# Expert stage: one more up-weight load on SyncE, and the last half's rows sent one tile earlier

## The chip, the cores and the metric

The kernel runs on one core of a Trainium2 chip. The metric is the device time of one execution in microseconds (us). Three executions of the kernel before took 436.18, 436.92 and 437.71 us, so the median is 436.92 us.

## What is computed

A transformer layer in float32 on x of 4 x 1024 rows by 128: causal attention with 16 heads and a latent of 32, a layer norm over x plus the attention, then a mixture of eight experts where each row goes to one expert only, and a second layer norm.

```python
x = _layernorm(x + attention(x))
gate_logits = einsum('bsd,ed->bse', x, gate_w) + gate_b + expert_bias
top_idx = argmax(gate_logits)
for e in range(8):
    h = relu(x @ w1[e] + b1[e])            # 128 -> 512
    y = h @ w2[e] + b2[e]                  # 512 -> 128
    out += (top_idx == e) * y
x = _layernorm(x + out)
```

## The kernel before

The engines run programs of their own, joined by semaphores: PE (TensorE), DVE (VectorE), ACT (ScalarE), POOL (GpSimd) and SP (SyncE, which only issues DMAs).

**Attention stage.** The loop over 144 units (`u`, 36 for each of the four batches) computes scores on PE, exponentials on ACT and clips on DVE. Between the units stand jobs for one half batch (512 rows) each: the output projection (`out`), the first layer norm and a transpose (`turnx`), the gate (`gate`) and `rank`, which gives each row its place in its expert's region of the DRAM tensor `by_expert`. After `rank`, POOL's `route` (L585) waits for `index_ready` and scatters the 512 rows of the half to `by_expert` with four indirect DMAs of 128 rows (L591).

**Expert stage.** It works through TILES = 39 tiles of 128 rows of one expert. The first EARLY_TILES = 17 tiles hold only rows of the first seven halves, so they need no row of the last half. The last half's own jobs (`out`, `turnx`, `gate`, `rank`) run inside the expert loop, at tiles 2, 5, 6 and 7 (`TAIL_AT`). The late tiles, 17 to 38, need all that follows from it: the four scatters of the last half, eight pad blocks written behind the regions (`pad`, L403: six by SP, two by ACT at tiles 8 and 9) and DVE's late plan of the tiles (tiles 7, 8, 9).

For tile `c`:

- SP's `load_tile` (L529, DMA at L535) fetches the 128 rows to one of 12 buffers `xs`; from tile 12 on it waits until the result of tile `c - 12` has been written.
- The up weights of the tile's expert (256 KB) go to one of six buffers `w1_tile`. In the kernel before, SP fetches those of tiles 0 to 4 during the attention stage (L539 to L542), ahead of its row loads, and ACT those of tile 5 on, five tiles ahead, with `load_up` (L1115, DMA at L1121): a value load of the expert's number, a wait for the buffer, the DMA.
- PE's loop at step `c` (L1381): `up_rows(c)` (L1350), `turn_x(c + 2)` (L1340), `down_rows(c - 1)` (L1367), then the tail job of that step.
- ACT's loop at step `c` (L1141): `relu(c)` (four activations, L1133), `xT_evac(c + 2)` (L1111), `load_up(c + 5)`, the tail job, and at steps 8 and 9 one pad. At step 0 it also empties the last attention sum (L1079). `relu` does the value load itself if `load_up` has not done it for that tile.
- DVE's loop (L1015): `residual` (L980), `y_sum` (L987), statistics (L993), `y_norm(c - 2)` (L1008), moments (L999, L1001), tail jobs, late plan.
- POOL's loop at step `c` (L622): `y_inverse_std(c - 1)` (L610), `write(c - 2)` (an indirect DMA to `out`, L618), and the routes that `ROUTE_AT` gives to this step. Each is in program order.

SP's order in the expert stage is: its five weight loads, row loads 0 to 16, six pads, the wait for all scatters, pads and the late plan (L546 to L549), row loads 17 to 38.

Of the kernel before, what the change touches and what calls it, by code (L numbers as in the profile page):

```python
# [126 lines left out]
def sums(b, pair, qc):  # L127
    return (b * PAIRS + pair) * NQC + qc
# [6 lines left out]
PLAN_AT = (7, 8, 9)  # L135

EARLY_PLAN_AT = (23, 24, 27, 28)
ROUTE_AT = {8: (0, 1), 9: (2, 3)}
PAD_AT = 8
PADS_ACT = 2  # L140
LAST_HALF = B * NQC - 1
# [2 lines left out]
def tail_job(c, kind=None):  # L144


    return [job for job in TAIL_JOBS if TAIL_AT.get(c) == job[0] and kind in (None, job[0])]
# [28 lines left out]
TILES = N // P + E - 1  # L176
# [5 lines left out]
W1_SLOTS = 6  # L182
W1_AHEAD = W1_SLOTS - 1
# [10 lines left out]
def build(nc, io):  # L194
    ctx = ExitStack()
    with ctx:
# [174 lines left out]
        def prob_ap(u, seg):  # L371
            _, _, off, w = seg
            return prob[u % P_SLOTS][:, :, off:off + w]
# [22 lines left out]
        def pad(eng, experts):  # L396


            eng.wait_ge(pad_ready, 1)
            eng.wait_ge(pad_in, 16)  # L400
            for e in experts:
                at = eng.value_load(pad_at[0:1, e:e + 1], min_val=0, max_val=DUMMY)
                eng.dma_start(by_expert[bass.ds(at, P), :], pad_row[:]).then_inc(padded, 16)  # L403
# [35 lines left out]
        def _(sp):  # L439
# [96 lines left out]

            sp.wait_ge(weighted, (B - 1) * UB)
            sp.wait_ge(scored, 2 * ((B - 1) * UB + NU))
            for c in range(W1_AHEAD):  # L539
                e = sp.value_load(expert_tab[0:1, c:c + 1], min_val=0, max_val=E - 1)  # L540
                sp.dma_start(w1_tile[c], io["w1"].rearrange("e d f -> (e d) f")[bass.ds(e * D, D), :]
                             ).then_inc(w1_in[c], 16)  # L542
# [11 lines left out]
        def _(pool):  # L554
# [15 lines left out]
            def inverse_std(g):  # L570
                pool.wait_ge(var_ready, g + 1)
                pool.tensor_tensor(rstd[g % Q][:], var_eps[g % Q][:], const[:, CONST["half"]], ALU.pow  # L572
                                   ).then_inc(rstd_ready, 1)
# [11 lines left out]
            def route(g, tiles):  # L585

                q = g % Q
                pool.wait_ge(index_ready, g + 1)
                pool.sem_inc(pool_seen, 1)
                for t in tiles:  # L590
                    pool.indirect_dma_start(by_expert, bass.IndirectOffsetOnAxis(ap=index[q][:, t:t + 1], axis=0),  # L591
                                            xrow[q][:, t, :], None).then_inc(routed[q], 16)
# [29 lines left out]
            for c in range(TILES + 2):  # L622
# [4 lines left out]
                if TAIL_AT.get(c) == "out":  # L627
                    inverse_std(LAST_HALF)
                if c in ROUTE_AT:
                    route(LAST_HALF, ROUTE_AT[c])  # L630
            for i in range(RING):
# [3 lines left out]
        def _(dve):  # L635
# [55 lines left out]
            def clip(u):  # L691

                _, segs = segments(u)
                p = prob[u % P_SLOTS]
                diag = UNITS[u % NU][1][0][1] * P >= UNITS[u % NU][0] * QC
                dve.wait_ge(exped, 2 * u + 2)
                if not diag:
                    dve.tensor_scalar(p[:], p[:], P_HI, P_LO, ALU.min, ALU.max).then_inc(clipped, 1)  # L698
                    return
                widths = [w for _, _, _, w in segs]  # L700
                if widths == [QC]:
                    on, off = p[:, :, 0:P], p[:, :, P:QC]
                    mask = mask_hi[:, 0, :].unsqueeze(1).to_broadcast([P, HG, P])
                elif widths == [P, 3 * P]:
                    on, off = p[:, :, 0:2 * P], p[:, :, 2 * P:QC]
                    mask = mask_hi[:].rearrange("p i q -> p (i q)").unsqueeze(1).to_broadcast([P, HG, 2 * P])
                else:
                    both = p[:].rearrange("p h (i s) -> p (h i) s", i=2)
                    on, off = both[:, :, 0:P], both[:, :, P:2 * P]
                    mask = mask_hi[:, 0, :].unsqueeze(1).to_broadcast([P, 2 * HG, P])  # L710
                dve.tensor_scalar(off, off, P_HI, P_LO, ALU.min, ALU.max)  # L711
                dve.scalar_tensor_tensor(out=on, in0=on, scalar=P_LO, in1=mask, op0=ALU.max, op1=ALU.min  # L712
                                         ).then_inc(clipped, 1)
# [327 lines left out]
        def _(act):  # L1041
# [32 lines left out]
            def o_evac(k):  # L1074

                act.wait_ge(weighted, last_unit(k) + 1)
                if k >= 2:
                    act.wait_ge(o_turned, k - 1)
                act.activation(o_sb[k % 2][:], o_acc[:], ACT.Copy).then_inc(o_out, 1)  # L1079

            def job(kind, i):
                if kind == "v":
                    v_evac(i)
                if kind == "turnx":
                    act.wait_ge(turnx_mm, i + 1)
                    act.activation(flipped[i % Q][:], misc[:], ACT.Copy).then_inc(turnx_out, 1)
# [19 lines left out]
            def xT_evac(c):  # L1106
                act.wait_ge(xs_turned, c + 1)
                if c >= 2:

                    act.wait_ge(up_mm, c - 1)  # L1110
                act.activation(xsT[c % 2][:], bank[c % 2][:, 0:P], ACT.Copy).then_inc(xsT_ready, 1)  # L1111
# [3 lines left out]
            def load_up(c):  # L1115


                experts[c] = act.value_load(expert_tab[0:1, c:c + 1], min_val=0, max_val=E - 1)
                if c >= W1_SLOTS:
                    act.wait_ge(up_mm, c - W1_SLOTS + 1)  # L1120
                act.dma_start(w1_tile[c % W1_SLOTS],  # L1121
                              io["w1"].rearrange("e d f -> (e d) f")[bass.ds(experts[c] * D, D), :]
                              ).then_inc(w1_in[c % W1_SLOTS], 16)

            def relu(c):

                e = experts.pop(c) if c in experts else act.value_load(expert_tab[0:1, c:c + 1], min_val=0, max_val=E - 1)
                act.wait_ge(up_mm, c + 1)
                if c >= 2:
                    act.wait_ge(down_mm, c - 1)  # L1130
                for f in range(DFF // P):
                    t = slice(f * P, (f + 1) * P)
                    last = act.activation(hiddenT[c % 2][:, t], bank[4 + c % 2][:, t], ACT.Relu,  # L1133
                                          bias=b1T[:, bass.ds(e * (DFF // P) + f, 1)])
                last.then_inc(hiddenT_ready, 1)
# [5 lines left out]
            for c in range(TILES):  # L1141
                relu(c)
                if c == 0:
                    o_evac(sums(B - 1, 1, 1))
                if c + 2 < TILES:
                    xT_evac(c + 2)
                if c + W1_AHEAD == EARLY_TILES:
                    act.wait_ge(planned, 4)
                if c + W1_AHEAD < TILES:
                    load_up(c + W1_AHEAD)  # L1150
                for kind, i in tail_job(c):
                    job(kind, i)
                if PAD_AT <= c < PAD_AT + PADS_ACT:
                    pad(act, [E - PADS_ACT + c - PAD_AT])
# [346 lines left out]
```

## Time and profile before

| | |
|---|---|
| median of three executions | 436.92 us |
| profiled execution, its own time | 439.81 us |
| its span (first to last instruction) | 438.1 us |
| PE busy | 406.7 us, 93% |
| DVE busy | 373.8 us, 85% |
| ACT busy | 351.6 us, 80% |
| POOL busy | 173.1 us, 40% |
| mean granted clock of PE | 0.977 |

The profiled execution lies 2.9 us above the median, and 1.7 us of it lie outside its span. Times within the trace are microseconds from the start of the span. A row of the timeline gives the start, the duration, the engine, the line of the program, the operation, output <- input and the number of instructions; the bracket gives the idle time of the engine before it and what ended it. `SPq` and `ACTq` are the DMA-issuing instructions of SP and ACT. The attention stage ends at about 341 us, the expert stage begins with the transposes at 338 us.

### The profile page before, as it was taken

To read this page: it belongs to the slowest core of one execution; us is meant where nothing else is said; L and a number is where in the kernel's file an instruction comes from. 1 tells how busy PE (TensorE), PEld (TensorE's weight loads), DVE (VectorE), ACT (ScalarE), POOL (GpSimd) and SP (SyncE) were. 2 spreads that over 40 slices of the span, in tenths; PEclk is the share of its full clock that TensorE was granted. 3 is DMA by queue.
4 is the path that set the end of the run, shared out by engine and by line. 5 is a ranking of instruction groups with operands and counts; after the bars stand their busy time and mean duration, and the time that the engine had idled before them with its cause. 6 is when DMAs were issued, how large, how long until landed. Compare 5 with 4: busy or idle time off the path is not lost. (4 is left out here: it accounts for less than half of the span.)

```text
span 438.1 us, 12095 instructions
## 1 busy us (share of the span) xinstructions
PE 406.7 (93%) x4139; PEld 222.8 (51%) x4139; DVE 373.8 (85%) x816; ACT 351.6 (80%) x560; POOL 173.1 (40%) x164
## 2 busy tenths in 40 slices
PE   8899999999999999899999999999998798699993
PEld 5533344444434354344344444343343697699993
DVE  3979799999999999979999999999998687367674
ACT  3879999999889989798899999989986464366662
POOL 8221001331553022507601322454001576678887
PEclk9889999999999999899999999999999999799998
DMA  5268501676066155401940760067214456567640
GB/s 154 54 170 196 155 1 49 145 176 194 2 160 181 49 114 125 104 1 30 211 101 1 170 151 21 2 145 197 72 41 121 116 156 173 145 175 214 189 139 19
DMA packets 33004, 50.60 MB, mean 116 GB/s; under 512 B 5627, under 2 KB 16545, under 8 KB 32944
## 3 DMA queue, kind: packets, MB, share of 16 engines
q1 hardware_dynamic: 25488, 36.51, 33.7%
q10 hardware_dynamic: 5184, 9.05, 7.2%
q0 software_dynamic: 2272, 4.27, 3.0%
q8 instruction: 34, 0.56, 0.5%
q14 instruction: 26, 0.21, 0.2%
HBM read 21.35 MB, written 5.33 MB: 61 GB/s over the span
## 5 line engine op out<-in xcount | busy, mean ns | idle before, releaser
L1048 ACT ACTIVATE prob<-ring 128x1024 f32<-128x1024 f32 x288 | 273.1, 1047 | 26.3 <-PE ring L1237 25.2
L1255 PE MATMUL o_acc<-prob,v_stat 128*32 128x512 f32 (+3 forms) x1536 | 156.0, 502 | 6.5 <-ACT o_sb L1079 5.1
L1237 PE MATMUL ring<-queries,keys 32*128 32x512 f32 (+3 forms) x1536 | 129.0, 384 | 3.6 <-DVE whole_q L658 3.0
L1237 PEld LDWEIGHTS ring<-queries,keys 32*128 32x128 f32 x1536 | 72.3, 186 | 88.7 <-issue 48.1
L698 DVE TENSOR_SCALAR prob<-prob 128x2048 f32<-128x2048 f32 x64 | 77.4, 1219 | 4.9 <-ACT prob L1048 4.6
L712 DVE SCALAR_TENSOR_TENSOR prob<-prob,mask_hi 128x1024 f32<-128x1024 f32 (+1 forms) x80 | 81.0, 1013 | 0.0
L1133 ACT ACTIVATE prob<-ring,b1T 128x128 f32<-128x128 f32 x156 | 44.5, 368 | 39.2 <-issue 17.8
L711 DVE TENSOR_SCALAR prob<-prob 128x1024 f32<-128x1024 f32 (+1 forms) x80 | 64.9, 811 | 4.0 <-ACT prob L1048 4.0
L1255 PEld LDWEIGHTS o_acc<-prob,v_stat 128*32 128x32 f32 x1536 | 34.4, 109 | 61.6 <-issue 42.4
L591 POOL DMA_INDIRECT by_expert<-xrow,index x32 | 43.5, 1360 | 46.0 <-DVE index L809 38.4
L572 POOL TENSOR_TENSOR rstd<-var_eps,const 128x4 f32<-128x4 f32 x8 | 17.1, 2134 | 92.4 <-DVE var_eps L757 92.4
L1367 PE MATMUL ring<-w,prob 128*128 x312 | 43.7, 285 | 7.8 <-ACT prob L1133 6.5
L581 POOL CAST key_parts<-whole_k 128x512 fp32r<-128x512 f32 x15 | 13.1, 875 | 87.6 <-ACT whole_k L1072 87.6
L1367 PEld LDWEIGHTS ring<-w,prob 128*128 128x128 f32 x312 | 39.6, 199 | 9.2 <-issue 9.1
L618 POOL DMA_INDIRECT out<-prob,queries x39 | 40.5, 1039 | 8.7 <-issue 8.7
L1350 PE MATMUL ring<-prob,v_stat 128*128 128x128 f32 x312 | 43.0, 282 | 0.3
L1350 PEld LDWEIGHTS ring<-prob,v_stat 128*128 128x128 f32 x312 | 38.9, 196 | 1.6 <-issue 1.6
L583 POOL CAST query_parts<-whole_q 128x512 fp32r<-128x512 f32 x15 | 29.1, 1939 | 12.8 <-DVE whole_q L658 12.8
L610 POOL TENSOR_TENSOR y_rstd<-y_var,const 128x1 f32<-128x1 f32 x39 | 22.9, 588 | 12.6 <-DVE y_var L1001 10.9
L993 DVE BATCH_NORM_STATS2 y_stats<-prob 128x6 f32<-128x128 f32 x39 | 11.5, 295 | 13.1 <-DVE prob L987 11.8
L987 DVE TENSOR_TENSOR prob<-ring,prob 128x128 f32<-128x128 f32 x39 | 11.3, 290 | 12.4 <-remote 6.2
L1202 PE MATMUL ring<-latent,w_kq 64*128 64x512 f32 x60 | 17.9, 674 | 0.9 <-DVE whole_q L667 0.5
(114 smaller groups left out, 330.2 us busy)
## 6 DMA issues: line engine op xcount, KB each, us to landing
queries<-query_parts SPq DMA_DIRECT2D x60, 256.0 KB, 4.0
v_stat<-in_w ACTq DMA_DIRECT2D x34, 256.0 KB
keys<-key_parts SPq DMA_DIRECT2D x60, 128.0 KB, 2.4
queries<-by_expert SPq DMA_DIRECT2D x39, 66.0 KB
xrow<-in_x_rows SPq DMA_DIRECT2D x8, 264.0 KB, 4.7
xT<-in_x_T SPq DMA_DIRECT2D x8, 256.0 KB, 3.1
v_stat<-in_w SPq DMA_DIRECT2D x5, 256.0 KB
out<-prob,queries POOLq DMA_INDIRECT x39
```

The source lines that it names most:

```text
L583: pool.tensor_copy(query_parts[i % 2][:, 0, :], whole_q[i % 2][:]).then_inc(upper_queries, 1)
L591: pool.indirect_dma_start(by_expert, bass.IndirectOffsetOnAxis(ap=index[q][:, t:t + 1], axis=0), xrow[q][:, t, :], None).then_inc(routed[q ...
L618: pool.indirect_dma_start(io["out"], bass.IndirectOffsetOnAxis(ap=xs[c % RING][:, D:D + 1].bitcast(U32), axis=0), zs[c % RING][:], None, b ...
L698: dve.tensor_scalar(p[:], p[:], P_HI, P_LO, ALU.min, ALU.max).then_inc(clipped, 1)
L711: dve.tensor_scalar(off, off, P_HI, P_LO, ALU.min, ALU.max)
L712: dve.scalar_tensor_tensor(out=on, in0=on, scalar=P_LO, in1=mask, op0=ALU.max, op1=ALU.min).then_inc(clipped, 1)
L1048: act.activation(prob[u % P_SLOTS][:, 2 * half:2 * half + 2, :].rearrange("p h s -> p (h s)"), slot(("score", u, half))[:], ACT.Exp, scale ...
L1133: last = act.activation(hiddenT[c % 2][:, t], bank[4 + c % 2][:, t], ACT.Relu, bias=b1T[:, bass.ds(e * (DFF // P) + f, 1)])
L1237: last = pe.matmul(out[:, j % 2 * QC + off:j % 2 * QC + off + w], keys[hg][r, kt * P:(kt + 1) * P], queries[hg][r, qc, part, QC - w:QC], s ...
L1255: last = pe.matmul(o_acc[j * VW:(j + 1) * VW, QC - w:QC], v_stat[b % 2][:, hg, kt, j, :], prob[u % P_SLOTS][:, j, off:off + w], start=begi ...
L1350: last = pe.matmul(bank[4 + c % 2][:, t], w1_tile[c % W1_SLOTS][:, t], xsT[c % 2][:], start=True, stop=True)
L1367: last = pe.matmul(bank[2 + c % 2][:, 0:D], hiddenT[c % 2][:, f * P:(f + 1) * P], w2_cols[:, bass.ds(e * DFF + f * D, D)], start=f == 0, s ...
```

## The change

SP fetches the up weights of six tiles (0 to 5) instead of five, ahead of its row loads. ACT's first `load_up` is that of tile 6, at step 1; at step 0 it issues none, and `relu(5)` does its own value load. POOL issues the last half's scatters 0 and 1 at step 7 and 2 and 3 at step 8, instead of steps 8 and 9. Nothing else is touched.

```diff
-ROUTE_AT = {8: (0, 1), 9: (2, 3)}
+ROUTE_AT = {7: (0, 1), 8: (2, 3)}
...
             sp.wait_ge(weighted, (B - 1) * UB)
             sp.wait_ge(scored, 2 * ((B - 1) * UB + NU))
-            for c in range(W1_AHEAD):
+            for c in range(W1_SLOTS):
                 e = sp.value_load(expert_tab[0:1, c:c + 1], min_val=0, max_val=E - 1)
                 sp.dma_start(w1_tile[c], io["w1"].rearrange("e d f -> (e d) f")[bass.ds(e * D, D), :]
                              ).then_inc(w1_in[c], 16)
...
                 if c + W1_AHEAD == EARLY_TILES:
                     act.wait_ge(planned, 4)
-                if c + W1_AHEAD < TILES:
+                if W1_SLOTS <= c + W1_AHEAD < TILES:
                     load_up(c + W1_AHEAD)
```

with W1_SLOTS = 6 and W1_AHEAD = 5.

## Rows read from the trace of the kernel before

**Rows 1.** Busy time by stretch: stretch, length, engines (instructions), granted clock, DMA share, GB/s

```profile
344.81:346.84 2.03, 0.00 (x0) 0.00 (x0) 0.63 (x3) 1.27 (x5) 0.33 (x1) 1.00 0.68 188
374.80:378.37 3.57, 0.00 (x1) 0.01 (x1) 1.07 (x6) 1.28 (x5) 1.31 (x2) 0.83 0.55 149
378.37:384.00 5.63, 5.63 (x26) 5.63 (x27) 2.85 (x14) 2.64 (x11) 4.85 (x6) 0.50 0.53 155
384.00:426.00 42.00, 42.00 (x376) 42.00 (x375) 29.26 (x132) 28.31 (x109) 34.36 (x44) 1.00 0.64 185
```

**Rows 2.** Timeline of PE and ACT at the start of the expert stage

```profile
341.67 1.13 PE L1350 MATMUL ring<-prob,v_stat 128*128 128x128 f32 x8
342.16 0.30 ACT L1111 ACTIVATE prob<-ring 128x128 f32<-128x128 f32 x1
342.83 2.04 ACTq L1121 DMA_DIRECT2D v_stat<-in_w  x1
344.54 0.27 PE L1340 MATMUL ring<-ident,queries 128*128 128x128 f32 x1
345.57 1.14 ACT L1133 ACTIVATE prob<-ring,b1T 128x128 f32<-128x128 f32 x4 [3.11 <-issue]
346.85 1.15 PE L1367 MATMUL ring<-w,prob 128*128 x8 [2.04 <-ACT prob L1133]
```

**Rows 3.** Line L1121, ACT's weight loads: duration in ns, minimum/median/maximum

```profile
L1121 ACTq DMA_DIRECT2D v_stat<-in_w x34: 14/344/2036, 342.8 to 420.6; - x34
```

**Rows 4.** Timeline of PE, ACT and DVE at steps 13 to 15

```profile
371.42 0.29 DVE L980 TENSOR_TENSOR prob<-queries,rope_q 128x128 f32<-128x128 f32 x1
373.55 1.13 PE L1350 MATMUL ring<-prob,v_stat 128*128 128x128 f32 x8
376.90 0.29 DVE L987 TENSOR_TENSOR prob<-ring,prob 128x128 f32<-128x128 f32 x1 [5.19 <-remote]
377.09 1.14 ACT L1133 ACTIVATE prob<-ring,b1T 128x128 f32<-128x128 f32 x4 [4.82 <-remote]
378.37 2.07 PE L1367 MATMUL ring<-w,prob 128*128 x8 [3.58 <-ACT prob L1133]
380.23 1.91 PE L1350 MATMUL ring<-prob,v_stat 128*128 128x128 f32 x8
384.82 0.27 PE L1340 MATMUL ring<-ident,queries 128*128 128x128 f32 x1
```

**Rows 5.** Timeline of POOL from its step 7 to its step 9

```profile
362.87 1.03 POOL L618 DMA_INDIRECT out<-prob,queries  x1 [0.26 <-issue]
365.68 0.57 POOL L610 TENSOR_TENSOR y_rstd<-y_var,const 128x1 f32<-128x1 f32 x1 [1.78 <-DVE y_var L1001]
367.85 1.02 POOL L591 DMA_INDIRECT by_expert<-xrow,index  x1 [0.30 <-issue]
370.15 0.58 POOL L610 TENSOR_TENSOR y_rstd<-y_var,const 128x1 f32<-128x1 f32 x1
373.52 0.96 POOL L591 DMA_INDIRECT by_expert<-xrow,index  x1 [0.30 <-issue]
```

**Rows 6.** Timeline of SP's pads and of its first late row load

```profile
365.92 0.37 SPq L403 DMA_DIRECT2D by_expert<-pad_row  x1
367.08 0.72 SPq L403 DMA_DIRECT2D by_expert<-pad_row  x1
...
376.85 0.33 SPq L403 DMA_DIRECT2D by_expert<-pad_row  x1
379.38 0.36 SPq L535 DMA_DIRECT2D queries<-by_expert  x1
```

**Rows 7.** SP's waits, and the register moves of line L403 in ns

```profile
SPq L548 <- DMA by_expert<-pad_row: 1.3, 1, 1.3
L403 SPq MOVE by_expert<-pad_row x6: 3/18/722, 365.9 to 376.8; - x6
```

**Rows 8.** Timeline: SP's early weight and row loads, PE's first transposes

```profile
325.62 5.19 SPq L541 DMA_DIRECT2D v_stat<-in_w  x5
331.58 33.50 SPq L535 DMA_DIRECT2D queries<-by_expert  x17
337.99 0.44 PE L1340 MATMUL ring<-ident,queries 128*128 128x128 f32 x2
```

**Rows 9.** All 32 scatters of L591, in ns; DVE's clip from the page; an index

```profile
L591 POOL DMA_INDIRECT by_expert<-xrow,index x32: 958/1322/2101, 94.2 to 373.5; - x32
L698 DVE TENSOR_SCALAR prob<-prob 128x2048 f32<-128x2048 f32 x64 | 77.4, 1219 | 4.9 <-ACT prob L1048 4.6
362.62 0.17 DVE L809 CAST index<-place_of 128x4 uint32<-128x4 f32 x1
```

## Prediction: what the change will do to the time

> **What bounds the kernel now.** I read the busy time by stretch first, then the timelines of single engines inside the stretches where PE is not full. From 384 to 426 us PE is busy without a gap at full clock, while ACT, DVE and POOL are busy for 67 to 82% of the time [rows 1]. So the late expert tiles are bound by PE: whatever time PE gains or loses before tile 17 reaches the end of the kernel in full. Two stretches ahead of that are empty on PE: 2.03 us at 344.81 and 3.57 us at 374.80 [rows 1]. The second is followed by 5.63 us of full work at half the granted clock, 0.50, the 1.2 GHz level [rows 1]. Only these two gaps and the clock behind the second can be won by a change at this place.
>
> The first gap ends when ACT has done `relu(1)`. ACT was not computing before that: it issued the weight load of tile 5, which took 2.04 us, and `relu(1)` could only start at 345.57 [rows 2]. The second gap ends with ACT's `relu(12)` at 377.09; DVE starts again at 376.90 [rows 4]. Both had their inputs long before (DVE stood for 5.19 us). In the same time SP's pads hardly move: the first two start 1.16 us apart, the sixth only at 376.85, and a mere register move of SP takes up to 722 ns [rows 6, 7]. So the sequencers of SP, ACT and DVE run slowly together while scatters, pads and loads are in flight, and no row says which of them does it. I cannot tell whether this slow stretch is as long in executions without the profiler; the profiled one is 439.81 us, 2.89 above the median. I therefore work out both cases.
>
> **Part A, the weight load of tile 5.** It removes one DMA issue and its value load from ACT's step 0. With the traced price, `relu(1)` can start once `up_rows(1)` is done at 341.67 + 1.13 = 342.80 instead of at 345.57, so it ends by about 344.0, before PE gets free at 344.81 [rows 2]. PE gains the whole gap, 2.0 us. That is the upper bound. Below: all 34 loads have a median issue of 0.344 us [rows 3]. With that, `relu(1)` would have started at 345.57 - (2.04 - 0.34) = 343.87 and ended at 345.01, and the gap would be 0.2 us. Since the 2.04 is the maximum of 34, I stay nearer to the median: 0.5 us. The load is not gone: tile 6's is now ACT's first, one step later. If it meets the same slow stretch, it delays `relu(2)`, but PE has `down_rows(1)` and the projection job of the last half in that time, so it costs PE nothing or at most the same 2.0 again.
>
> What SP takes over: one more load in front of its row loads. Five loads took 5.19 us, some 1.2 us each from start to start [rows 8]. All row loads shift by 1.2 us; the first is issued at 331.58 and needed at 337.99, 6.4 us later [rows 8], which covers it. Without that cover it would cost up to 1.2 us. `relu(5)` now does a value load of its own, 345.57 - (342.83 + 2.04) = 0.70 us by the same step before `relu(1)` [rows 2]. PE's transposes of the last half at step 5 cover it; uncovered it is 0.7 us, once.
>
> **Part B, the scatters one step earlier.** The index is ready at 362.79 [rows 9]. POOL is at `write(5)` from 362.87 to 363.90 and then idles 1.78 us until 365.68 [rows 5]. Scatters 0 and 1 move into that hole and past it: with 0.30 us before each, scatter 0 runs 364.20 to 365.2 and scatter 1 365.5 to 366.5. `y_inverse_std(7)` (0.57) follows, ends at 367.1 and not 366.25; `write(6)` 367.3 to 368.3; scatter 2 368.6 to 369.6; scatter 3 starts at 369.9 instead of 373.52 [rows 5]. So the last scatter is issued 3.6 us earlier. Queued behind them: `y_inverse_std(8)`, at 370.9 instead of 370.15. DVE's `y_norm(8)` waits for it, 0.7 us late, and PE's down matmul needs that buffer only two tiles later; the cover is about 1.9 us a tile, and DVE is idle for 5 us soon after [rows 4].
>
> What it is worth depends on what the late tiles wait for. SP waits for pads 1.3 us, and its first late row load goes out at 379.38 [rows 6, 7]. In the trace the pads are last, made so by the slow stretch. At the pace of the first two, the sixth pad would start at 365.92 + 5 x 1.16 = 371.7, and land some 1.6 us after (as 376.85 + 0.33 + 1.3 = 378.5 shows), at 373.4 [rows 6, 7]. Scatter 3, issued until 374.48, has landed by 378.5: between 1.6 us (as a pad) and 4.0 us after. So without the slow stretch the scatters are last, at 376.1 to 378.5; the row load follows 0.9 us later and lands like a pad 1.6 us after, at 378.6 to 381.0. A step of PE is 1.9 us (42.00 us for 376 matmuls, 17 a step [rows 1]), so PE would come to the transpose of tile 17 after `up_rows(15)`, at about 373.55 + 2 x 1.9 + 1.0 = 378.3, a little earlier if steps 11 to 13 are not slowed, and wait for it 0.3 to 3.6 us, 2.3 with its steps 1 us earlier and the middle of the landings. With the slow stretch, the gap is the 3.57 us of the trace. The earlier scatters close either gap but for a rest, by 3.6 us at most. Between 2.3 and 3.6 I take 3.0 us. If pads alone held the gap, it would be 0.
>
> **The clock.** After the gap 26 matmuls run at 0.50; a group of eight takes 1.91 us rather than 1.13 [rows 4]. 5.63 us at half speed cost 2.8 us. A gap of 2.03 us did not bring the clock down [rows 1]. If the second gap shrinks to under 1 us, the nearest row says that all 2.8 are won; but in executions where the gap is shorter than traced the clock may not fall before either, and then it is 0. I take half, 1.4 us.
>
> **A rule that speaks against B.** The last scatter of the stage is issued in 0.96 us [rows 5], but the median over all 32, most of them beside DVE's clips of 1.22 us, is 1.32 and the longest 2.10 [rows 9]. The Trainium skill (page "SBUF — State Buffer", section "SBUF: two separate sides") says that GpSimd cannot write DMA descriptors while VectorE runs an operation that takes both ports. The spread of the scatters agrees with it. At step 7 the neighbours on DVE are the late plan's small operations, so by the row at hand (0.96) there is no loss; by 2.10 each, four scatters take 4.6 us longer and the 3.6 us are gone. The Trainium skill (page "DMA: Bandwidth & Descriptors", section "Issuing engines are not separate DMA queues") also says that transfers of all issuing engines interleave on the same 16 DMA engines; the stage from 364 us on is then the worst place for the scatters, since pads and loads are there. That is the slower rival below.
>
> **Sum.** 0.5 + 3.0 + 1.4 = 4.9 us off the median, 432.0 us. From the profiled execution with its own prices: 439.81 - 2.0 - 3.0 - 2.8 = 432.0 as well. The most is 2.0 + 3.6 + 2.8 = 8.4, hence 428.5. This is the forecast, chance 0.67, with 428.5 to 434.5 as its own range.
>
> **Rivals.** (1) The pads are the last wait and the slow stretch is theirs. Then the scatters land earlier and nobody notices: row load 17 still goes out at about 379.4 and ACT and DVE start again at 376.9. Only A stays, 0.2 to 2.0 us: 434.9 to 436.7, say 436.2. For it: SP's only wait there is for pads. Against it: POOL's scatters span most of the same time. Chance 0.18. (2) The issue of the scatters is stretched beside DVE: scatter 3 comes no earlier, 436.4 us. Chance 0.05. (3) Slower: the earlier scatters meet the pads and row loads 15 and 16, the slow stretch of the sequencers starts with scatter 0 at 364.2 instead of at 367.1 and still ends at 376.9. Then `relu(9)` and `relu(10)` are late too, and PE loses up to 2.9 us more, less A: 436.92 + 2.4 = 439.3. It decides as soon as the stretch grows by more than A gives, 0.5 us. For it: the stretch starts with the second pad, not with a scatter. Chance 0.10. (4) A only passes its 2.04 us issue on to the next load: A is 0, and the forecast becomes 432.5; inside its range.
>
> **Numbers.** About 0.3%, 1.3 us, is what a measurement of this kernel can tell from no change. Faster by more than that (below 435.6): the forecast's 0.67 and the best part of rival 1, 0.08, together 0.75. Same: the rest of rival 1 and rival 2, 0.15. Slower: 0.10. The range goes from 428.5 to 436.5, which leaves out rival 3 and the tails.
>
> **What would show it.** A: no load from ACT between 342 and 344 us, `relu(1)` by 343.5, the gap at 344.8 under 0.5 us. B: scatter 3 issued near 370 less A; SP's wait before the first late row load ends by 376; PE's gap near 375 below 1 us. Clock: no stretch at 0.50 after it. I am wrong if that row load still goes out near 379, if ACT and DVE stand for 5 us again, or if the half clock comes back although the gap is shorter.

## The result, and the profile after

The changed kernel took 434.50 us (median; 432.79 to 438.40), the kernel before 437.16 us in the same comparison. The ratio is 0.9948, 95% interval 0.9924 to 0.9972: a gain of 2.3 us, with 1.2 to 3.3 inside the interval. I had forecast 4.9 us. The direction and the range held; the forecast size was about twice what came. The ratio isn't the quotient of the two medians (that is 0.9939, or 2.7 us), and the same holds for the runs below; where two times are compared directly, they are given.

All ratios below are to the kernel before on the same chip, because the chips differ: the kernel before took 438.0 and 436.6 us on the first two chips of the experiments and 431.1 to 431.4 us on the last two.

The profiled execution of after took 435.73 us with a span of 434.0, against 438.1 before; before's profiled execution, at 439.81 us, was one of its slower ones. The difference lies ahead of the expert stage. The first `up_rows` matmul starts at 335.14 us rather than at 339.36, and the last `down_rows` matmul starts 91.78 us later (91.69 before). The two lines of the page that show why, first of before:

```profile
PEclk9889999999999999899999999999999999799998
```

and of after, each digit the granted clock in one of 40 slices:

```profile
PEclk9999999999999999999999999999999999799997
```

Before lost clock in slices 2, 3 and 17, in code that the change doesn't touch; after did not. Two profiled spans would have said "4.1 us faster, nearly as forecast", and for the wrong reason. The expert stage must be read step by step. Windows of after that answer to [rows 1] (window, length, engines, clock, DMA share, GB/s):

```profile
348.97:349.80 0.83, 0.00 (x1) 0.03 (x1) 0.83 (x4) 0.83 (x5) 0.55 (x2) 1.00 0.77 253
363.67:369.13 5.46, 0.00 (x0) 0.01 (x1) 2.68 (x12) 1.28 (x5) 3.55 (x4) 0.88 0.39 124
369.13:374.60 5.47, 5.47 (x25) 5.47 (x26) 2.38 (x11) 2.65 (x11) 3.19 (x4) 0.50 0.59 157
380.00:422.00 42.00, 41.71 (x369) 41.49 (x370) 28.46 (x129) 28.23 (x109) 34.59 (x44) 1.00 0.66 187
```

The gap of 2.03 us at the start of the stage is gone. The gap of 3.57 us came back as one of 5.46, and the half clock behind it is there again. The start of the stage in after, which answers to [rows 2]:

```profile
338.86 1.15 ACT L1133 ACTIVATE prob<-ring,b1T 128x128 f32<-128x128 f32 x4 [0.61 <-PE ring L1350]
340.19 0.59 ACTq L1121 DMA_DIRECT2D v_stat<-in_w  x1
340.41 1.06 PE L1367 MATMUL ring<-w,prob 128*128 x8
```

`relu(1)` runs 3.7 us after the first matmul of the stage; in before it was 6.2. ACT's first load, now that of tile 6, costs 0.59 us and nobody waits for it. Part A works. Now the middle of the stage, which answers to [rows 4 to 6]:

```profile
359.38 0.96 POOL L591 DMA_INDIRECT by_expert<-xrow,index  x1 [0.31 <-issue]
364.64 7.46 SPq L403 DMA_DIRECT2D by_expert<-pad_row  x6
365.00 0.96 POOL L591 DMA_INDIRECT by_expert<-xrow,index  x1 [0.30 <-issue]
366.81 0.02 ACTq L403 DMA_DIRECT2D by_expert<-pad_row  x1
367.85 1.14 ACT L1133 ACTIVATE prob<-ring,b1T 128x128 f32<-128x128 f32 x4 [6.58 <-remote]
369.13 2.07 PE L1367 MATMUL ring<-w,prob 128*128 x8 [5.46 <-ACT prob L1133]
376.98 2.70 SPq L535 DMA_DIRECT2D queries<-by_expert  x3
```

Scatters 0 and 3 go out at 359.38 and 365.00: counted from the first matmul of the stage, 4.3 us earlier than before. But ACT stands for 6.58 us while the scatters go out (`remote`: it was released by an event that the profile ties to no instruction). From 358.66 to 366.94 SP gets on only in steps of 0.65 to 0.74 us, with one to three instructions in each, whatever they are; in before this slow stretch ran from 367.06 to 376.9. It moved along with the scatters. It doesn't begin with them, though: its first slow instruction starts 0.8 us (before) and 0.7 us (after) ahead of scatter 0, while POOL issues the write to `out` that stands ahead of it. And SP's row load of tile 17, which had to come earlier, is issued 41.84 us after the first matmul of the stage, against 40.02 before. What SP waited for ahead of it:

```profile
SPq L548 <- DMA by_expert<-pad_row: 4.0, 1, 4.0
```

Line 548 is the wait for the pads. It took 1.3 us in [rows 7], now 4.0, and there is no wait for scatters.

### The profile page after: what moved, and what is told of

Its sections match the earlier page's. It is cut to its first block and busy times, and to the rows that moved or that the text cites. A ratio compares the mean times of both kernels' runs of the same rounds, so it can differ in the third digit from the quotient of the medians.

```text
span 434.0 us, 12098 instructions
## 1 busy us (share of the span) xinstructions
PE 403.0 (93%) x4139; PEld 221.9 (51%) x4139; DVE 373.1 (86%) x816; ACT 351.3 (81%) x560; POOL 173.2 (40%) x164
## 5 line engine op out<-in xcount | busy, mean ns | idle before, releaser
L1255 PE MATMUL o_acc<-prob,v_stat 128*32 128x512 f32 (+3 forms) x1536 | 153.7, 495 | 5.2 <-ACT o_sb L1079 3.8
L591 POOL DMA_INDIRECT by_expert<-xrow,index x32 | 43.5, 1359 | 46.0 <-DVE index L809 38.4
L572 POOL TENSOR_TENSOR rstd<-var_eps,const 128x4 f32<-128x4 f32 x8 | 17.1, 2136 | 89.6 <-DVE var_eps L757 89.6
L581 POOL CAST key_parts<-whole_k 128x512 fp32r<-128x512 f32 x15 | 14.1, 940 | 85.7 <-ACT whole_k L1072 85.7
L583 POOL CAST query_parts<-whole_q 128x512 fp32r<-128x512 f32 x15 | 28.1, 1874 | 12.8 <-DVE whole_q L658 12.8
L1202 PE MATMUL ring<-latent,w_kq 64*128 64x512 f32 x60 | 16.9, 641 | 1.0 <-DVE whole_q L667 0.5
```

What stands on the lines that cost most here:

```text
L583: pool.tensor_copy(query_parts[i % 2][:, 0, :], whole_q[i % 2][:]).then_inc(upper_queries, 1)
L1255: last = pe.matmul(o_acc[j * VW:(j + 1) * VW, QC - w:QC], v_stat[b % 2][:, hg, kt, j, :], prob[u % P_SLOTS][:, j, off:off + w], start=begi ...
```

## The experiments

The expectations name theories by a letter; each says what its letter stands for.

### One part alone

`e1_load_only`: part A. Scatters stay at tiles 8 and 9.

```diff
-ROUTE_AT = {7: (0, 1), 8: (2, 3)}
+ROUTE_AT = {8: (0, 1), 9: (2, 3)}
```

> Part A alone: SyncE fetches tile 5's up weights, scatters stay at steps 8 and 9. Theory M (the slow stretch of the sequencers moves with the scatters, so part B gains nothing and part A is the whole gain): ratio to before 0.993 to 0.997, some 2 us faster, the PE gap near 344 gone and the gap near 372 as before, about 3.6 us. Rival B (the gain is that of the earlier scatters): ratio 0.998 to 1.001.

Measured: ratio 0.9954 (0.9916 to 0.9993), the whole gain of the change. The early gap is gone. The later gap is there in two pieces, 1.43 and 2.81 us, with 3.4 us at half clock behind them. Scatter 3 starts 33.5 us after the stage's first matmul, where before has 34.2 and after 29.9: of after's 4.3 us, part B's own share is 3.7.

`e2_scatter_only`: part B. SP loads five tiles' weights, ACT the sixth, as before.

```diff
-            for c in range(W1_SLOTS):
+            for c in range(W1_AHEAD):
...
-                if W1_SLOTS <= c + W1_AHEAD < TILES:
+                if c + W1_AHEAD < TILES:
```

> Part B alone: scatters at steps 7 and 8, ScalarE still fetches tile 5's up weights. Theory M: ratio 0.998 to 1.003; the slow stretch begins about 3.5 us earlier than in the kernel before and falls on ScalarE's second pad, PE's second gap is 5 us or more instead of 3.6. Rival B: ratio 0.993 to 0.996 and the second gap under 2 us.

Measured: ratio 0.9995 (0.9952 to 1.0039), nothing that can be told from zero: the interval goes from a gain of 2.1 us to a loss of 1.7. With ACT's load of tile 5 back, the early gap is back too:

```profile
339.58 2.48 ACTq L1121 DMA_DIRECT2D v_stat<-in_w  x1
344.03 1.15 PE L1367 MATMUL ring<-w,prob 128*128 x8 [2.49 <-ACT prob L1133]
...
370.61 1.14 ACT L1133 ACTIVATE prob<-ring,b1T 128x128 f32<-128x128 f32 x4 [7.32 <-remote]
371.89 2.07 PE L1367 MATMUL ring<-w,prob 128*128 x8 [6.20 <-ACT prob L1133]
```

The issue took 2.04 us in [rows 2], 2.48 here and 2.22 in `e11_before_finish6`; those are all the traces that have it at step 0. So its 2 us are its price at this place. The median of 34 loads, to which I had leaned, says nothing about it.

### Who makes the slow stretch

`e3_all_at_7`: all four scatters at step 7.

```diff
-ROUTE_AT = {7: (0, 1), 8: (2, 3)}
+ROUTE_AT = {7: (0, 1, 2, 3)}
```

> The changed kernel with all four scatters at step 7. If the slow stretch lasts from the first to just after the last scatter and is made by GpSimd's DMAs back to back, it shrinks from 8.2 us to some 6 us (two writes fewer in between), PE's second gap from 5.5 us to about 3, and the time falls by 1 to 3 us against the changed kernel (ratio to before 0.988 to 0.993). If the stretch belongs to the pads, it stays at 8 us or more and the time does not fall (0.995).

Measured: 0.9971 (0.9932 to 1.0009). Scatter 3 starts 28.0 us after the stage's first matmul instead of 29.9 in after; the row load of tile 17 at 41.4 instead of 41.8. Sending it still earlier buys next to nothing.

`e4_pads_sp`: SP sends all eight pads, since one of ACT's two fell into its stall.

```diff
-PADS_ACT = 2
+PADS_ACT = 0
```

> The changed kernel with all eight pads issued by SyncE, none by ScalarE. Theory: in the changed kernel ScalarE's second pad, five slow sequencer instructions of about 0.72 us, holds relu(10) for some 3.7 us; without it PE's second gap falls from 5.5 to about 2 us, but SyncE's pads end about 2.2 us later and the first late row load with them, so PE waits again at tile 17; net 0 to 3 us faster than the changed kernel, ratio to before 0.988 to 0.995. Rival (ScalarE's stall has nothing to do with its pad): PE's gap stays above 4.5 us.

Measured: 0.9993 (0.9954 to 1.0033). PE's gap became 7.00 us; ACT's stall stayed without a pad of its own. The pad on ACT isn't its cause.

`e5_spaced`: one scatter at every second step.

```diff
-ROUTE_AT = {7: (0, 1), 8: (2, 3)}
+ROUTE_AT = {7: (0,), 9: (1,), 11: (2,), 13: (3,)}
```

> The changed kernel with one scatter each at steps 7, 9, 11 and 13 instead of two each at 7 and 8. Theory Q (the slow stretch lasts as long as GpSimd has a DMA queued behind a running one): the stretch breaks into pieces of some 2.5 us each, PE's gap near 364 falls from 5.5 to under 2.5 us; but the last scatter comes at about 374 and the first late row load with it near 379, so PE waits some 3 us at tile 17 and the time is within 1.5 us of the changed kernel (ratio to before 0.993 to 1.000). Rival (the stretch comes with any scatter and the pads, of 8 us): one unbroken stretch of 8 us and a gap of 5 us remain.

Measured: 1.0027 (0.9991 to 1.0064). The slow stretch breaks into short pieces (361.8 to 363.0, 368.6 to 370.1), but now tile 17 waits for the last scatter, issued at 378.67:

```profile
SPq L549 <- DMA by_expert<-xrow,index: 5.3, 1, 5.3
384.23 0.48 PE L1340 MATMUL ring<-ident,queries 128*128 128x128 f32 x1 [8.26 <-DMA queries<-by_expert]
```

`e6_pads_after`: SP sends all eight pads, and only once the scatters have landed.

```diff
-PADS_ACT = 2
+PADS_ACT = 0
...
-            pad(sp, range(E - PADS_ACT))
             for q in range(Q):
                 sp.wait_ge(routed[q], B * QT * 16)
+            pad(sp, range(E - PADS_ACT))
```

> The changed kernel with all eight pads on SyncE and only after the four scatters have landed, so that pads and scatters never overlap. Rival P (the slow stretch is the pads' collision with the scatters): no slow stretch, PE's gap near 364 gone, then one wait of 6 us or so at tile 17 because the pads end near 379. Theory Q: the stretch and the 5 to 7 us gap remain, and the wait at tile 17 comes on top: slower than before, ratio 1.000 to 1.010.

Measured: 1.0084 (1.0043 to 1.0124), slower since the pads are late. What it was made for:

```profile
361.21 0.96 POOL L591 DMA_INDIRECT by_expert<-xrow,index  x1 [0.30 <-issue]
368.66 1.14 ACT L1133 ACTIVATE prob<-ring,b1T 128x128 f32<-128x128 f32 x4 [6.53 <-remote]
369.94 2.07 PE L1367 MATMUL ring<-w,prob 128*128 x8 [5.34 <-ACT prob L1133]
370.06 9.32 SPq L403 DMA_DIRECT2D by_expert<-pad_row  x8
```

ACT's stall and PE's gap have the size that they have in after, and the first pad is issued after both. Pads don't make the slow stretch. Of what these runs moved, it follows the scatters. POOL's writes to `out` stand between and ahead of the scatters in all of them and were not varied, so the scatters alone are not shown to be the cause.

`e7_landed`: POOL waits for each scatter's landing before it sends the next.

```diff
-                    route(LAST_HALF, ROUTE_AT[c])
+                    pool.wait_ge(written[c - 2], 16)
+                    for t in ROUTE_AT[c]:
+                        route(LAST_HALF, [t])
+                        pool.wait_ge(routed[LAST_HALF % Q], ((B - 1) * QT + t + 1) * 16)
```

> The changed kernel in which GpSimd waits, before the first scatter of a step and after each scatter, until its last DMA has landed. Theory Q and the theory that too many row writes are in flight at once both expect no slow stretch, PE's gap near 364 under 1.5 us and the clock at full speed behind it; the four scatters take 3.5 us each, ending near 374; ratio to before 0.985 to 0.993. If the stretch stays 8 us long, neither holds.

Measured: 1.0141 (1.0097 to 1.0185). SP's pads keep a pace of 1.1 us, so the stretch is gone, but POOL comes so late that PE has gaps of 6.27 and 5.97 us and runs 17.1 us at the lower clock.

`e8_finish`: before and after each scatter POOL writes one element to a tile that nobody reads and waits until it is done, which costs 0.6 us a time. I call it the marker.

```diff
+            def finish():
+                pool.memset(mark[:], 0.0).then_inc(marked, 1)
+                marks.append(1)
+                pool.wait_ge(marked, len(marks))
...
-                    route(LAST_HALF, ROUTE_AT[c])
+                    finish()
+                    for t in ROUTE_AT[c]:
+                        route(LAST_HALF, [t])
+                        finish()
```

> The changed kernel in which GpSimd runs a one-element memset and waits for it before the first scatter of a step and after each scatter: the next DMA instruction is not queued while one runs, but the scatters still follow each other within some 1.8 us and are in flight together. Theory Q: the slow stretch goes or falls under 3 us, PE's gap near 364 under 1.5 us, ratio to before 0.983 to 0.991. Theory F (row writes in flight): the stretch stays 8 us and the gap about 5 us, ratio 0.993 to 0.998.

Measured: 0.9875 (0.9825 to 0.9926), the best ratio of all, with no slow stretch in the trace. It looked like a cure. The next job took it apart.

### The same on another chip

`e9_finish_8_9` is `e8` with the scatters at tiles 8 and 9. `e10_finish_all` is `e8` with the marker behind each scatter of half 6 too (the seventh half, whose scatters run as the expert stage begins). `e11_before_finish6` is the kernel before with the marker behind half 6's scatters alone. `e12_pairs` is `e8` with POOL's writes of tiles 18 and later two at a time.

```diff
+                if 2 <= c < 20 or c == TILES + 1:
+                    write(c - 2)
+                elif c >= 20 and c % 2:
+                    write(c - 3)
```

> The kernel with the finish marker, but the last half's scatters at steps 8 and 9 as in the kernel before. Is the earlier place worth something once the slow stretch is gone? If the argument of part B holds there (first late row load waits for the scatters): the last scatter comes near 374.5 instead of 371, the first late row load near 380, PE waits 2 to 4 us at tile 17; 1.5 to 4 us slower than with scatters at 7 and 8, ratio to before 0.991 to 0.997. If the place does not matter: ratio 0.985 to 0.990.

> The marker kernel with markers between the scatters of the seventh half too (those that run while the expert stage begins). The slow stretch near 338 to 342 goes as well. Since ScalarE issues no weight load there any more, PE gains at most the 0.5 to 1.5 us gaps of that stretch: ratio to before 0.983 to 0.990, the same as or up to 1 us better than with markers in the last half alone.

> The kernel before, with markers between the scatters of the seventh half and no other edit: ScalarE still issues tile 5's load at step 0. If part A gained because that load fell into the slow stretch made by queued scatters, the issue takes 0.35 instead of 2.04 us, PE's 2.0 us gap near 344 falls to 0.3 us or less, and this kernel gains what part A gained: ratio 0.994 to 0.998. If the load's issue is long for another reason, it stays near 2 us and the ratio is 0.999 to 1.002. The second stretch near 367 to 377 is untouched in both cases.

> The marker kernel in which, from tile 18 on, GpSimd issues its writes in pairs, back to back, every second step. No scatter and no pad is near. If it is a DMA queued behind a running DMA on GpSimd that slows the others, SyncE's instructions show steps of 0.72 us in the steady part and PE gets gaps there: 2 to 15 us slower than the marker kernel, ratio to before 0.992 to 1.02. If scatters or pads are needed, the steady part stays at 1.9 us a tile without gaps, ratio 0.985 to 0.990.

Measured: `e9` 0.9980 (0.9963 to 0.9997), `e10` 0.9957 (0.9939 to 0.9975), `e11` 1.0006 (0.9979 to 1.0032), `e12` 1.0131 (1.0097 to 1.0165). `e9` and `e10` gained less than expected. The surprise is `e11`: the last half's scatters stand side by side without a marker, and there is no slow stretch. The kernel before took 431.4 us on this chip rather than 436.6. So a chip, or a moment, can lack the stretch without any marker, and what `e8` owed to its marker is open again: on its chip `e5` and `e6` had the stretch, but they differ from it in more than the marker, and the changed kernel itself was not timed beside it.

`e11` also settles what it was made for. Half 6's scatters are spaced and no slow stretch is near, and yet ACT's load of tile 5 is as long to issue as before:

```profile
335.86 2.22 ACTq L1129 DMA_DIRECT2D v_stat<-in_w  x1
```

(L1129 is L1121, moved down by the edit.) Here its price comes neither from queued scatters nor from the stretch, and not from SP's issues beside it either: SP's row loads at 335.74 and 336.84 us take their usual 0.34 us while ACT stands in its own. `e12` has no slow stretch either. From tile 17's transpose to the last `down_rows` it takes 48.9 us, where `e9` to `e11` take 46.3 to 46.7, and from there to the end of the span 11.9 for 7.1. In this case late writes in pairs cost time without a slow stretch.

### Four kernels on one chip

Part A is in all four; with or without part B, with or without the marker at the scatters of half 6 and of the last half. No new edits: `e13_after` is the changed kernel, `e14_load_only` is `e1` again, `e15_finish_all` is `e10` again, and `e16_finish_all_8_9` is `e15` with the scatters at tiles 8 and 9.

> The changed kernel itself, beside three others on one chip. Four kernels form a square: scatters at tiles 7 and 8 or at 8 and 9, with or without a one-element memset of POOL, awaited, before and after every scatter of the last half's and half 6's rows (the marker). All four hold part A. Theory F (B is worth nothing in time, wherever it is tried): e13_after and e14_load_only within 0.3% of each other, both 0.5% (2.0 to 2.3 us) below before. Theory G (B is worth something, and the slow stretch that follows the scatters takes it back): e13_after within 0.3% of e14_load_only, but e15_finish_all 0.4% or more below e16_finish_all_8_9.

> Part A alone, no marker. All theories: 0.9955 of before, 2.0 us, as the traced issue of tile 5's weights on ACT (2.0 to 2.5 us). If it lies above 0.998, the value found for A in the first job was chance.

> Parts A and B with the marker around the scatters of half 6 and of the last half. Theory M (the marker ends the slow stretch of the sequencers): no SP or ACT instruction stretched to 0.72 us behind the last half's scatters, stage no longer than 88 us, and 0.4% or more below e13_after of the same chip. Theory C (the slow stretch belongs to a chip or to a moment, and the marker does nothing): e15 within 0.3% of e13_after, and both traces show the stretch, or neither.

> Part A with the marker, scatters at tiles 8 and 9. Theory M: below e14_load_only by 0.4% or more. Theory C: within 0.3% of it. Theory G: above e15_finish_all by 0.4% or more, since the last scatter is issued later and tile 17 waits for it; theory F: within 0.3% of it.

| | scatters at 7, 8 (A and B) | scatters at 8, 9 (A alone) |
|---|---|---|
| no marker | `e13` 428.73 us, 0.9933 (0.9905 to 0.9961) | `e14` 428.27 us, 0.9946 (0.9925 to 0.9967) |
| marker | `e15` 429.70 us, 0.9966 (0.9943 to 0.9989) | `e16` 431.20 us, 1.0005 (0.9986 to 1.0023) |

Down the columns: by the medians the marker costs 1.0 and 2.9 us, and theory M's gain did not come. But none of the four traces has the slow stretch that the marker was to end, so M's mechanism was not tested here. The stretch belongs to the chips, or to the moments, of the first two jobs; what the marker does there stays open. Along the rows: without marker B brings nothing that can be measured (theory F). With it, the scatters come later and B brings 1.5 us, about what theory G expected, but not for G's reason: there is no stretch in any of the four that could take it back. B's worth depends on how late the scatters are against what lands next.

The two undisturbed traces show where B goes. `e14_load_only`, scatters late: SP's waits, the last scatter, POOL's late statistics, the row load of tile 17, PE's wait for it:

```profile
SPq L548 <- DMA by_expert<-pad_row: 3.4, 1, 3.4
SPq L549 <- DMA by_expert<-xrow,index: 2.5, 1, 2.5
...
357.49 6.22 SPq L403 DMA_DIRECT2D by_expert<-pad_row  x6
366.27 0.95 POOL L591 DMA_INDIRECT by_expert<-xrow,index  x1 [0.30 <-issue]
367.86 0.40 DVE L1008 TENSOR_SCALAR prob<-prob,y_mean,y_rstd 128x128 f32<-128x128 f32 x1 [2.68 <-POOL y_rstd L610]
370.47 9.19 SPq L535 DMA_DIRECT2D queries<-by_expert  x8
372.98 0.33 PE L1340 MATMUL ring<-ident,queries 128*128 128x128 f32 x1 [1.48 <-DMA queries<-by_expert]
```

`e13_after`, scatters early:

```profile
SPq L548 <- DMA by_expert<-pad_row: 3.3, 1, 3.3
...
359.29 6.67 SPq L403 DMA_DIRECT2D by_expert<-pad_row  x6
363.28 0.96 POOL L591 DMA_INDIRECT by_expert<-xrow,index  x1 [0.30 <-issue]
370.22 8.44 SPq L535 DMA_DIRECT2D queries<-by_expert  x8
373.28 0.33 PE L1340 MATMUL ring<-ident,queries 128*128 128x128 f32 x1 [2.75 <-DMA queries<-by_expert]
```

Line 549 is, in the source, the wait for the late plan; the instruction that stands under it waits for the last half's scatters as well, behind the one for the pads. In `e14` the plan was done at 362.1 us and the last scatter lands last: SP goes through line 548 at 367.1 and then waits 2.5 us, until 369.6. In `e13` the wait for scatters is gone, as forecast. But the last pad, issued until 365.96, lands 3.3 us later, at 369.3, so it took the scatter's place 1.1 us after the scatter's landing (368.17). Counted from the stage's first matmul, the scatter is issued 3.9 us earlier (28.7 for 32.6), and the row load 1.2 us (35.6 for 36.8). PE's gaps: 1.27 + 1.47 = 2.74 us in `e14`, one of 2.75 in `e13`. The first of `e14`'s two gaps is closed by B. It came from POOL's `y_inverse_std`, late behind the scatters: DVE's `y_norm` waited 2.68 us for it, `y_sum` stands behind that, and `down_rows` waits for an earlier `y_sum` to free its bank. But two short gaps have become one long, and behind the long one the clock falls:

```profile
370.53:373.28 2.75, 0.00 (x1) 0.00 (x1) 2.14 (x10) 1.14 (x4) 2.54 (x3) 1.00 0.53 159
373.28:375.40 2.12, 2.12 (x12) 2.00 (x13) 0.29 (x1) 0.28 (x1) 1.70 (x3) 0.73 0.55 120
```

and in `e14`, where it stays at its upper level:

```profile
367.97:369.24 1.27, 0.00 (x1) 0.00 (x1) 0.99 (x5) 1.24 (x5) 1.21 (x2) 1.00 0.67 194
371.51:372.98 1.47, 0.00 (x0) 0.00 (x0) 1.16 (x6) 1.14 (x4) 1.29 (x2) 1.00 0.52 136
373.00:415.00 42.00, 42.00 (x373) 41.70 (x374) 29.43 (x132) 27.81 (x106) 35.94 (x45) 1.00 0.67 184
```

`e13` runs 3.4 us at half clock from 374.3 on, which costs 1.7. The timed executions fit: the mean granted clock was 0.984 to 0.992 in all seven of `e13`, and 0.996 or 0.997 in five of `e14`'s twelve; 0.004 of 428 us is 1.7. It reaches tile 17's transpose 38.66 us after the stage's first matmul, `e14` 39.27, but from there to the last `down_rows` it takes 48.10 for 46.54. Gain 0.6, loss 1.6. That B's gain is lost to the clock rests on these two traces.

### The pads ahead of two row loads

If the pads are now last, they should be sent earlier.

```diff
-            for c in range(EARLY_TILES):
+            for c in range(EARLY_TILES - 2):
                 load_tile(c)
             pad(sp, range(E - PADS_ACT))
+            for c in range(EARLY_TILES - 2, EARLY_TILES):
+                load_tile(c)
```

`e17_pads_before_15` has parts A and B, `e18_load_pads_15` part A alone.

> The changed kernel, with SP's six pads ahead of row loads 15 and 16 instead of behind them (2.3 us earlier, by two loads at 1.15 us). Theory L (after the scatters were moved, the pads landed last; in e13_after's trace the last pad landed at 369.29 us and the last scatter at 368.17, in e14_load_only's the last pad at 367.06 and the last scatter at 369.63): now the scatters land last again, row load 17 goes out about 1.1 us earlier after the stage's start than the 35.6 us of e13_after, PE's wait for tile 17's rows shrinks from 2.75 to about 1.6 us, and the kernel comes 0.9 to 1.5 us (0.2 to 0.35%) below 0.9933 of before, and below e18. Theory N (the wait for tile 17 is not on the path, or DMA sharing makes scatters and pads land at the same time in any order): row load 17 within 0.3 us of 35.6 and the time that of e13_after. Slower: row loads 15 and 16, 7 us later, delay the transposes 15 and 16.

> Part A alone (scatters at tiles 8 and 9), with the six pads ahead of row loads 15 and 16. Theory L: the scatters are last here as without the move (36.8 us after the stage's start), so the time is that of e14_load_only, 0.9946 of before, and 0.2 to 0.35% above e17. Theory N: equal to e17 too.

Measured: `e17` 428.18 us, 0.9939 (0.9912 to 0.9967); `e18` 428.22 us, 0.9937 (0.9912 to 0.9962). No difference. The two rows that count in `e17`, SP's wait for scatters (line 551) and PE's long wait:

```profile
SPq L551 <- DMA by_expert<-xrow,index: 0.2, 1, 0.2
368.14 0.33 PE L1342 MATMUL ring<-ident,queries 128*128 128x128 f32 x1 [2.40 <-DMA queries<-by_expert]
```

and in `e18`:

```profile
SPq L551 <- DMA by_expert<-xrow,index: 4.0, 1, 4.0
366.57 0.33 PE L1342 MATMUL ring<-ident,queries 128*128 128x128 f32 x1 [2.01 <-DMA queries<-by_expert]
```

The order came out as theory L has it: in `e17` the scatters are last again, by 0.2 us, and B is worth 3.0 us at the row load (33.5 for 36.4 after the first matmul). Theory L's time didn't come. PE now waits 2.40 and 2.01 us for row load 15, which stands behind the pads: the case "slower" of the expectation, paid with what was won. The clock falls again for 3.4 us in `e17` and not in `e18`. An order of SP's queue that serves tiles 15 and 17 alike was not tried.

## Why the prediction was half right

The sum was 0.5 + 3.0 + 1.4 us. What came is 2.0 to 2.3 us from part A and nothing that can be measured from part B and from the clock. The two errors have opposite signs, so the total is off by less than part B and the clock are, and that the range held is in part luck.

**Part A.** The mechanism was right, the term mis-sized. I took 0.5 us between 0.2 and 2.0. The runs show 2.0 us (`e1`), 2.3 (`e14`) and 2.7 (`e18`, with its pads moved), the upper bound or more. Three traces have the load at step 0, and all three show 2.0 to 2.5 us for its issue. The failed step is "since the 2.04 is the maximum of 34, I stay nearer to the median": the maximum was the first of them, at the one place that counts. Its cover worked: ACT's next load took 0.59, 1.11 and 0.80 us in after, `e14` and `e13`, where nobody waits for it. Rival 4 falls.

**Part B, the issue.** As worked out: scatter 0 in POOL's hole behind `write(5)`, 0.96 us each, the fourth 3.7 us earlier than in `e1` and 3.9 earlier than in `e14`, where I had 3.6. Its rival, an issue stretched beside DVE, did not come. The rule of the Trainium skill ("SBUF — State Buffer", "SBUF: two separate sides") stood beside that rival; at 0.96 us a scatter this place doesn't show it.

**Part B, the worth, with the slow stretch.** I took 3.0 us. The step that failed in the kernels that the forecast was measured on is "the earlier scatters close either gap but for a rest". It held the slow stretch in its place while the scatters moved. But the stretch moved with them: PE's gap of 3.58 us came back as one of 5.46, and row load 17 went out 41.8 us after the first matmul and not 40.0. `e2`, part B alone, has no gain (0.9995), and its interval leaves out 3.0 us. Why the stretch moves along stays open.

**Part B, the worth, without it.** Here the failed step is "without the slow stretch the scatters are last, at 376.1 to 378.5". That is right for late scatters (`e14`), and it named what lands last then, not what lands next. I had put the pads at 373.4, from a landing 1.6 us after the start of the issue, 1.3 after its end. In `e13` and `e14` the last pad lands 3.7 us after the start, 3.3 to 3.4 after the end, and in `e13` that is 1.1 us behind the scatters. The Trainium skill ("DMA: Bandwidth & Descriptors", "Issuing engines are not separate DMA queues") says that such transfers interleave on the same engines; a longer landing agrees with it, although no run here separates the two. Of 3.9 us only 1.2 reached the row load, and in time `e13` against `e14` and `e17` against `e18` show nothing. The landing of row load 17 was too short in my sum as well: I had 1.6 us from the start of its issue to its landing; to PE's transpose the traces show 3.1 (`e13`) and 2.5 (`e14`). And the wait of 2.3 us at tile 17 is 2.5 by my own terms (379.8 less 377.3).

**Rival 1** (the pads are the last wait and the slow stretch is theirs, only A stays, 434.9 to 436.7) had a chance of 0.18 and comes nearest: with A at its full 2.0 us it gives 434.9, and 434.5 was measured. The pads were the last wait in after. Its other half, that the slow stretch belongs to the pads, fell with `e6`, and row load 17 did not stay where it was.

**Rival 3** (the stretch starts with scatter 0, earlier, and still ends at 376.9) was half right too. In before and after the stretch did start within 0.8 us of scatter 0. But it also ended earlier, at 366.94 and not at 376.9: it moved as a whole, 9.8 us long before and 8.3 after. So PE's gap was not closed but shifted, and even grew.

**The clock.** 1.4 us were to come from a gap too short to bring the clock down. The gap did not shrink, so neither did this term: 6.8 us at half clock in before and in after. On the undisturbed chips the term has the other sign: `e13` has 3.4 us of it where `e14` has none.

**Kept in doubt.** I could not tell whether the slow stretch is there in each execution. It is not there in each trace: the ten of the last two chips don't have it. Executions without a trace can't show it.

## What to carry to other kernels

When a wait covers several transfers, work out when each lands and not only the last; moving that one is worth the distance to the next, and to whatever stands behind it in the queue. Price an instruction by the row at its own place in the program; a maximum that is also the first of its kind need not be an outlier. When a wait seems to come from a slow stretch, ask whether the stretch moves along with what you move. And don't compare two profiled spans: here their whole difference of 4.1 us lay ahead of the stage that the change is about.

## What the runs showed of the hardware

- In the traces of before and after and of `e1` to `e4` and `e6`, SP gets on only in steps of about 0.72 us for 8 to 10 us (`e6`: for 4.4 us, then it waits), even at a register move. ACT stands for 4.1 to 8.2 us in them while PE's results are long there. `e5` has the stretch in pieces, `e7` and `e8` don't have it. None of the ten traces of the other two chips has it, `e13`, which is the changed kernel, included.
- The traces of before, after and `e1` to `e8` hold 3,375 to 3,656 records of finished DMAs, those of the other two chips 4,795 to 4,902, for nearly the same transfers. `e7` and `e8` have few records and no stretch, so the count goes with the chips rather than with the stretch. Whether recording has a part in the stretch was not tried.
- The first weight load that ACT issues took 2.04, 2.48 and 2.22 us at step 0; where the first one is at step 1, 0.39 to 1.26. The cause was not isolated.
- The length of PE's gap alone doesn't say whether the clock falls behind it. In the middle of the stage it stayed at the 2.4 GHz level after gaps of 1.27, 1.47 and 2.01 us (`e14`, `e18`). It fell to 1.2 GHz for 3.4 us after 2.25, 2.40 and 2.75 (`e15`, `e17`, `e13`), and for 6.8 us after 3.58 and 5.46 (before, after). At the start of the stage it stayed after 2.28 and 2.49 us (`e11`, `e2`).
